# A four-layer graph network on one core: fewer barriers between the first two convolutions, and a rearranged final stage

## What is computed

```python
h = sage_mean(x, src, dst, W_self1, W_neigh1, b1, n)   # x @ W_self + mean of neighbours @ W_neigh + b
h = relu(h)
h = sage_mean(h, src, dst, W_self2, W_neigh2, b2, n)   # the second convolution
...
# last layer, agg being the sum of the neighbours' rows
h = (1.0 + gin_eps[0]) * x + agg
h = h @ W.T + b
mean = jnp.mean(h, axis=0)
var = jnp.mean(jnp.square(h - mean), axis=0)
h = gamma * (h - mean) * jax.lax.rsqrt(var + BN_EPS) + beta
h = jax.nn.relu(h) + x
out = layernorm(x + h)                                  # so twice x is added to the relu
```

## Time and profile before

| what | us |
|---|---|
| median of three runs | 1755.76 |
| their range | 1755.16 to 1755.86 |
| the profiled execution | 1752.44 |
| its span, first to last instruction | 1750.3 |
| PE busy | 1468.5 |
| DVE, ACT, POOL busy | 760.0, 668.9, 784.7 |

### The profile page before, as it was taken

How to read it: one execution, slowest core, us unless ns; L and a number is a source line. 1 busy time by engine, 2 the same in 40 slices (tenths; PEclk the granted TensorE clock), 3 DMA queues, 4 the chain that set the end, 5 groups by cost and what they waited for, 6 DMA issues and landing times.

```text
span 1750.3 us, 31633 instructions
## 1 busy us (share of the span) xinstructions
PE 1468.5 (84%) x9759; PEld 1049.2 (60%) x9872; DVE 760.0 (43%) x2792; ACT 668.9 (38%) x1236; POOL 784.7 (45%) x819
## 2 busy tenths in 40 slices
PE   1789999969986877888888888889888988957996
PEld 1346666644545766676666666667666766634554
DVE  6997888622333322233334334323433343235445
ACT  3765555520002433344335334434433453321111
POOL 4300000000003777777777777777777777710000
PEclk9999999989997999989999999999999999969998
DMA  2000000001005333333333333333333333300001
GB/s 78 1 0 1 2 1 1 2 25 38 0 0 158 98 82 82 82 86 83 82 80 87 83 82 80 88 79 85 84 82 82 83 86 82 74 11 1 1 1 38
DMA packets 158697, 95.81 MB, mean 55 GB/s; under 512 B 120584, under 2 KB 143879, under 8 KB 158607
## 3 DMA queue, kind: packets, MB, share of 16 engines
q0 software_dynamic: 25088, 51.43, 11.4%
q1 hardware_dynamic: 133519, 43.21, 10.0%
HBM read 87.24 MB, written 7.32 MB: 54 GB/s over the span
## 4 chain that ended last, share of the span: by engine, by line
PE 31%; DMA 11%; POOL 9%; issue 8%; DVE 5%; ACT 2%; DVEq 2%; SPq 1%; POOLq 0%; ACTq 0%
DMA arena<-x_w1a,idx 9%; POOL arena L751 9%; PE ps L1077 6%; PE ps L1217 6%; PE ps L1086 5%; PE ps L1070 4%; PE ps L1058 3%; PE ps L1066 3%; PE ps L1127 1%; PE ps L1201 1%; DVE arena L1986 1%; DVEq L328 1%; DMA arena<-in_edge_attr 1%; DVE idx L1955 1%; ACT arena L1490 1%
## 5 line engine op out<-in xcount | busy, mean ns | idle before, releaser
L751 POOL DMA_INDIRECT arena<-x_w1a,idx x784 | 742.3, 947 | 692.2 <-issue 651.9
L1480 ACT ACTIVATE arena<-ps 88x512 f32<-88x512 f32 x196 | 116.3, 594 | 478.9 <-PE ps L1058 473.4
L1086 PEld LDWEIGHTS ps<-arena 128*128 128x128 f32 x1568 | 208.4, 195 | 111.5 <-issue 74.0
L1066 PE MATMUL ps<-ident_f,arena 128*128 128x128 f32 x784 | 132.6, 294 | 110.4 <-DMA arena<-x_w1a,idx 109.7
L1986 DVE TENSOR_TENSOR arena<-ps,bias_b 128x512 f32<-128x512 f32 x196 | 135.6, 692 | 204.6 <-PE ps L1077 204.6
L1981 DVE TENSOR_TENSOR arena<-win_i,late 128x96 f32<-128x96 f32 x196 | 51.4, 262 | 391.5 <-PE ps L1086 380.7
L1077 PE MATMUL ps<-w_c,arena 128*128 128x128 f32 x1568 | 221.3, 287 | 0.0
L1319 ACT ACTIVATE adj<-ps 128x300 f32 x392 | 172.5, 450 | 125.2 <-PE ps L815 118.1
L1070 PE MATMUL ps<-arena 88*128 88x512 f32 x392 | 208.3, 613 | 3.7 <-ACT arena L1480 3.7
L1077 PEld LDWEIGHTS ps<-w_c,arena 128*128 128x128 f32 x1568 | 204.4, 203 | 0.2
L1086 PE MATMUL ps<-arena 128*128 128x24 f32 x1568 | 197.0, 264 | 5.3 <-ACT arena L1490 2.9
(11 more groups left out here) (187 smaller groups left out, 1447.0 us busy)
## 6 DMA issues: line engine op xcount, KB each, us to landing
arena<-in_edge_attr SPq DMA_DIRECT2D x196, 128.0 KB, 2.5
arena<-x_w1a,idx POOLq DMA_INDIRECT x784
arena<-x_w1b SPq DMA_DIRECT2D x196, 12.0 KB
x_spill<-arena SPq DMA_DIRECT2D x1, 1600.0 KB, 7.2
x_w1a<-arena SPq DMA_DIRECT2D x6, 256.0 KB, 2.3
x_w1b<-arena SPq DMA_DIRECT2D x6, 256.0 KB, 2.6
arena<-x_spill SPq DMA_DIRECT2D x6, 256.0 KB, 2.8
out_x<-arena SPq DMA_DIRECT2D x3, 512.0 KB
```

Source lines behind the costliest of these rows:

```text
L751: pool.indirect_dma_start(out=z_e[v][:, j * D:(j + 1) * D], out_offset=None, in_=xa_d[:, :], in_offset=bass.IndirectOffsetOnAxis(ap=idx[:, ...
L1066: pe.matmul(z_t[:, j * P:(j + 1) * P], z_e[v][:, j * P:(j + 1) * P], ident_f[:, :], is_transpose=True, start=(j == 0), stop=False)
L1086: last = pe.matmul(ps[:, WIN_BANK[v % 2], 0:WIN], msg[:, j * P:(j + 1) * P], oh_e[v][:, j, :], start=(j == 0), stop=(j == J - 1))
```

## The change

At the seam: barriers 2 and 3 move into the If body. In the Else body the steps run on semaphores alone: PE's sums of chunk 6 and the two linear steps come behind the branch, the split of `xn` is written out chunk by chunk on ACT (`h_hi`, `h_mid`) and DVE (`h_less_hi`, `h_low`) with buffers of its own (`res_1`), with the relus and combines of chunks 5 and 6 between them. The flag's transpose goes to bank 0 after the first 24 terms of chunk 5's sums, the square root of the degrees comes earlier on ACT, `late` is reloaded when the adjacency is written, the second weights and bias are loaded when PE and DVE no longer need the first ones, and the loop of conv 2 has its first pair written out.

At the end: batch-norm rows go to `z_t` (the memory of `acc`), so that `xn` stays; barrier 8 is gone. Each chunk has a PSUM bank of its own, and PE adds twice the fp32 rows with one matmul a chunk (`twice_x`) as soon as that bank is read. Relu goes by chunks, statistics by chunks, and of a pair's two chunks DVE normalizes the first and ACT the second.

```diff
-            for n in range(1, 3):
-                phase_end(sp, n)
+            phase_end(sp, 1)
+            sp.wait_ge(adj_written, counted(ROUNDS))
...
+            with sp.Else():
+                sp.wait_ge(c1_lin, NC)
+                second_weights()
+                sp.wait_ge(c1_done, NC)
+                second_bias()
+                sp.wait_ge(res_ready, 2 * NC)
+                sp.sem_inc(phase_ends, 2)
             load_nodes(xn, t["x"], loads[3])
             phase_end(sp, 4)
...
-            phase_end(sp, 8)
-
             for g, (k0, nt) in enumerate(PAIR):
-                sp.wait_ge(out_ready, g + 1)
+                sp.wait_ge(out_ready, min(2 * g + 2, NC))
...
-            c1_sum(EARLY, ALL_TERMS)
+            c1_sum(EARLY, ALL_TERMS[:24])
             pe.wait_ge(off_ready, 1)
-            pe.transpose(ps[0:1, 3, 0:P], off[:, 0:1], ident_f[:, :]).then_inc(off_t, 1)
+            pe.transpose(ps[0:1, 0, 0:P], off[:, 0:1], ident_f[:, :]).then_inc(off_t, 1)
+            c1_sum(EARLY, ALL_TERMS[24:])
             for c in (EARLY, EARLY + 1):
                 for j in range(CHUNKS[c][1]):
                     c1_own(c, j)
-            c1_sum(EARLY + 1, ALL_TERMS)
-            c1_linear(EARLY)
-            c1_linear(EARLY + 1)
-            phase_end(pe, 2)
...
             def sage(call, c, nt):
                 n0 = call * NC
+                pe.wait_ge(loads[4], 48 * (call + 1))
...
+                c1_sum(EARLY + 1, ALL_TERMS)
+                c1_linear(EARLY)
+                c1_linear(EARLY + 1)
+                layer(1, sage, aggregate, peeled=1)
+                pe.sem_inc(phase_ends, 2)
             phase_end(pe, 4)
...
-            phase_end(pe, 8)
-
             pe.wait_ge(twice_ready, 1)
-            for g, (k0, nt) in enumerate(PAIR):
-                pe.wait_ge(bn_relu, g + 1)
-                if g >= 2:
-                    pe.wait_ge(out_ready, g - 1)
+
+            def twice_x(c):
+                k0, nt = CHUNKS[c]
+                pe.wait_ge(gin_out, c + 1)
+                pe.matmul(ps[:, c, 0:nt * D], twice_i, xn[:, k0:k0 + nt, :].rearrange("p k d -> p (k d)"),
+                          start=True, stop=False)
+
+            def add_bn(c):
+                k0, nt = CHUNKS[c]
+                pe.wait_ge(bn_relu, c + 1)
                 for j in range(nt):
-                    k = k0 + j
-                    o = ps[:, 2 * (g % 2) + j // CH, (j % CH) * D:(j % CH + 1) * D]
-                    for q in range(3):
-                        pe.matmul(o, ident_h[:, :], parts[q][:, k, :], start=(q == 0), stop=False)
-                    last = pe.matmul(o, agg_all[:, k * P:(k + 1) * P], ident_f[:, :], start=False, stop=True)
+                    last = pe.matmul(ps[:, c, j * D:(j + 1) * D], z_t[:, (k0 + j) * P:(k0 + j + 1) * P], ident_f[:, :],
+                                     start=False, stop=(j == nt - 1))
                 last.then_inc(fin_ready, 1)
+
+            for c in range(4):
+                twice_x(c)
+            for c in range(NC):
+                add_bn(c)
+                if c + 4 < NC:
+                    twice_x(c + 4)
...
+            act.wait_ge(deg_ready, 1)
+            act.activation(std_deg[:, :], dinv[:, :], ACT.Sqrt).then_inc(deg_ready, 1)
             c1_copy(EARLY, 1)
             c1_copy(EARLY, 0)
             c1_copy(EARLY + 1, 0)
-            c1_copy(EARLY + 1, 1)
-            act.wait_ge(deg_ready, 1)
-            act.activation(std_deg[:, :], dinv[:, :], ACT.Sqrt).then_inc(deg_ready, 1)
-            c1_relu(EARLY)
-            c1_relu(EARLY + 1)
-            phase_end(act, 2)
...
+            def h_hi(c):
+                k0, nt = CHUNKS[c]
+                act.wait_ge(c1_relued, c + 1)
+                act.activation(parts[0][:, k0:k0 + nt, :], xn[:, k0:k0 + nt, :], ACT.Copy).then_inc(hi_ready, 1)
+
+            def h_mid(c):
+                k0, nt = CHUNKS[c]
+                act.wait_ge(res_ready, NC + c + 1)
+                act.activation(parts[1][:, k0:k0 + nt, :], res_1[c % 2][:, 0:nt, :], ACT.Copy).then_inc(mid_ready, 1)
...
+            with act.Else():
+                act.sem_inc(self_out, NC)
+                c1_copy(EARLY + 1, 1)
+                act.wait_ge(c1_own_ready, NC)
+                h_hi(0)
+                h_hi(1)
+                h_mid(0)
+                h_mid(1)
+                for c in range(2, EARLY):
+                    h_hi(c)
+                for c in range(EARLY, NC):
+                    c1_relu(c)
+                for c in range(2, EARLY):
+                    h_mid(c)
+                for c in range(EARLY, NC):
+                    h_hi(c)
+                    h_mid(c)
+                act.sem_inc(phase_ends, 2)
...
-            phase_end(act, 8)
-
-            for k0, nt in PAIR:
-                act.activation(agg_all[:, k0 * P:(k0 + nt) * P], agg_all[:, k0 * P:(k0 + nt) * P], ACT.Relu,
+            act.wait_ge(cols_ready, 2)
+            for k0, nt in CHUNKS:
+                act.activation(z_t[:, k0 * P:(k0 + nt) * P], z_t[:, k0 * P:(k0 + nt) * P], ACT.Relu,
                                bias=cols[:, 6:7], scale=cols[:, 5:6]).then_inc(bn_relu, 1)
-            for k0, nt in PAIR:
+            for g, (k0, nt) in enumerate(PAIR):
                 root(nt)
+                if nt == 2 * CH:
+                    act.wait_ge(fin_norm, g + 1)
+                    for j in range(CH, nt):
+                        last = act.activation(xn[:, k0 + j, :], ps[:, 2 * g + 1, (j - CH) * D:(j - CH + 1) * D], ACT.Identity,
+                                              scale=rstd[:, j:j + 1], bias=nbias[:, j:j + 1])
+                    last.then_inc(out_ready, 1)
...
+                h_less_hi(0)
+                h_less_hi(1)
+                h_low(0)
+                h_low(1)
+                c1_combine(EARLY)
+                c1_combine(EARLY + 1)
+                for c in range(2, NC, 2):
+                    some = range(c, min(c + 2, NC))
+                    for n in some:
+                        h_less_hi(n)
+                    for n in some:
+                        h_low(n)
...
+                dve.tensor_scalar(twice_i, ident_f[:, :], 2.0, None, ALU.mult).then_inc(twice_ready, 1)
...
-            phase_end(dve, 8)
-
-            dve.tensor_scalar(ident_h[:, :], ident_h[:, :], 2.0, None, ALU.mult).then_inc(twice_ready, 1)
+            dve.tensor_tensor(cols[:, 6:7], cols[:, 2:3], rstd[:, 1:2], ALU.subtract).then_inc(cols_ready, 1)
+
+            def rows_of(c, nt):
+                return ps[:, c, 0:nt * D].rearrange("p (j d) -> p j d", d=D)
+
             for g, (k0, nt) in enumerate(PAIR):
-                dve.wait_ge(fin_ready, g + 1)
-                b = 2 * (g % 2)
-                layernorm(ps[:, b:b + 2, :].rearrange("p a (j d) -> p (a j) d", d=D), xn[:, k0:k0 + nt, :], nt, done=out_ready)
+                halves = [(2 * g, CH), (2 * g + 1, CH)] if nt == 2 * CH else [(2 * g, nt)]
+                for c, n in halves:
+                    dve.wait_ge(fin_ready, c + 1)
+                    for j in range(n):
+                        own.add(dve.bn_stats(stats[:, CH * (c - 2 * g) + j, :], rows_of(c, n)[:, j, :]))
+                own.wait()
+                if g:
+                    dve.wait_ge(out_ready, 2 * g)
+                for j in range(nt):
+                    last = dve.bn_aggr(mv[:, j, :], stats[:, j, :])
+                last.then_inc(var_ready, 1)
+                roots[0] += 1
+                dve.wait_ge(std_ready, roots[0])
+                own.add(dve.reciprocal(rstd[:, 0:nt], std[:, 0:nt]))
+                own.wait()
+                if nt == 2 * CH:
+                    dve.scalar_tensor_tensor(out=nbias[:, 0:nt], in0=mv[:, 0:nt, 0], scalar=-1.0, in1=rstd[:, 0:nt],
+                                             op0=ALU.mult, op1=ALU.mult).then_inc(fin_norm, 1)
+                c, n = halves[0]
+                for j in range(n):
+                    last = dve.tensor_scalar(xn[:, k0 + j, :], rows_of(c, n)[:, j, :], mv[:, j, 0:1], rstd[:, j:j + 1],
+                                             ALU.subtract, ALU.mult)
+                    if j < n - 1:
+                        own.add(last)
+                last.then_inc(out_ready, 1)
```

More of the change, by code:

```diff
@@ L731, in _ @@
             with pool.If_ne(flag, 0):
+                phase_end(pool, 2)
                 for n in (1, 2):
@@ L736, in _ @@
                 scan(pool, X, scan_tile)
-            phase_end(pool, 3)
-            with pool.If_ne(flag, 0):
+                phase_end(pool, 3)
                 scan(pool, H, scan_tile)
+            with pool.Else():
+                pool.sem_inc(phase_ends, 2)
             phase_end(pool, 4)
@@ L1438, in relu_pair @@
                     p0, pt = PAIR[g]
[L1439 to L1451 removed]
+                    act.activation(xn[:, p0:p0 + pt, :], node[:, 0:pt, :], ACT.Relu).then_inc(c1_relued, 1)
             def root_pair(times):
@@ L1458, in root_pair @@
                 return roots_of
-            split(1)
```

(38 more changed lines are left out.)

81 lines of the change are left out of this document (42 added, 39 removed).

## The result

| | before | after |
|---|---|---|
| median, us (four runs of each, side by side) | 1755.46 | 1733.12 |
| their range | 1752.97 to 1755.86 | 1732.42 to 1739.08 |
| the profiled execution | 1752.44 | 1732.96 |
| its span | 1750.3 | 1730.8 |

The forecast had 1736.7 (1730 to 1742.5).

What follows compares the result with a forecast made beforehand. Most of the span is the untouched edge loop, so time before and after it counts one for one. Savings of 11.8 + 7.3 = 19.1 us from the profiled 1752.44 give 1733.3; plus 3.3 for the median, 1736.7 (range 1730 to 1742.5).

Steps and rivals of the forecast that it cites:

- The seam: Between convolutions 1 and 2: 11.8 us saved, conv 2 starting at 384.85 at full clock against 396.66.
- Run-ahead: PE's sequencer runs 17 matmuls ahead at the seam, reaching the flag load at 370.05, 1.2 us ahead.
- Rival A: At the seam PE's jump is hidden by a longer queue, with no idle or half clock: 1731.1, chance 0.17.
- Price of the jump: PE's branch between the rows and chunk 6's sums costs 3.97 us, the late transfer being out of its way.
- Half clock: PE's restart behind the jump loses 2.0 us in the sums of chunk 6, with ends 0 and 4.35.
- The chain to conv 2: After chunk 6's sums: ACT's copy and high part, DVE's residuals, the low part, with gaps 3.2 us.
- The stall for low part 2: Early in conv 2, low part 2 comes some 0.4 us after PE wants it; 0.4 added.
- The end: Final stage behind batch norm's last factor: early doublings, chunk-wise steps and ACT's share save 7.3 us.
- Rival C: PE runs the end at half clock, chunk 1 at 1730.7 rather than 1724.95: 5.8 lost, 1742.5, chance 0.06.
- B: Slow seam restart: jump 5.74, chunk 6's sums and conv 2's first 16 matmuls at half clock; 1743.6, chance 0.17.
- D: Conv 2 stays at half clock, 0.22 us more per 512-column matmul; 1769.7 at a third of them; chance 0.02.
- E: At the seam SP's queue (weights, bias, x) holds conv 2 back; only 7.3 is left, 1748.5, chance 0.03.

Runs made afterwards that it cites:

- e0: The changed kernel run again with no edit, beside before on one chip: 1734.08 us, ratio 0.9891.
- e1: Only the hunks between the convolutions, against the kernel before, with the final stage as before: 1740.72 us, ratio 0.9938.
- e6: The changed kernel, but the doubling of each chunk waits for ACT's relu of that chunk: 1736.54 us, ratio 0.9902 to before.
- e7: The changed kernel, but DVE normalizes both chunks of a pair and ACT has no share: 1738.44 us, ratio 0.9908 to before.
- e4: The kernel before with one edit: SP starts the late reload when the adjacency is written, ahead of barrier 2: 1751.32 us, ratio 0.999.
- e3_jump_early: The changed kernel with PE's flag load and jump moved ahead of 25 of chunk 5's last 50 sums: 1726.70 us, ratio 0.9857 to before.
- e5: The changed kernel with the late reload started so that it runs during PE's jump: 1734.01 us, ratio 0.9895 to before.
- e2_end: Only the hunks of the final stage, against the kernel before, with barriers 2 and 3 kept: 1743.16 us, ratio 0.9954.

## Why the prediction was right, point by point

**The seam** was forecast at 11.8 us. In the first profile it is 23.54 - 11.19 = 12.35 of the distance and 18.84 - 16.37 = 2.47 in conv 2's first matmuls, 14.8. Over the five profiles in which the seam is as the change has it (after, e0, e1, e6, e7) the distance is 12.33 on the mean, so the gain 13.7. Of it the reload's way out of the jump accounts for 1.85 (e4); the rest came with the barriers and the new order of the steps, which no run took apart. The steps:
- *Run-ahead.* Load at 370.05 expected, 369.84 seen; the 17 matmuls hold, and e3_jump_early shows the queue a second time. Rival A falls by this. TensorE: Matmul & The Clock Gate in the Trainium skill gives the queue 64 entries; here the sequencer stood 18 matmuls ahead, 36 instructions with their weight loads, which is less, and no run shows what set this number.
- *Price of the jump.* Taken as 3.97; it was 3.32 to 3.86 in these five. The step of choosing between the rows by the reload was right (e4, e5); the term was 0.1 to 0.65 too high. Advanced Engine Details and Errata, section Control Flow Timing, in the Trainium skill has 108 ns for a compare-and-branch; none of the twelve jumps of the table comes near.
- *Half clock.* Taken as 2.0, with 0 and 4.35 as ends. It was 0 in two of the five and 1.62 in three. This is the mis-sized term for the first profile; for the kernel it was a fair value, only not a constant.
- *The chain to conv 2.* 3.2 us expected from the end of the sums to conv 2, 3.1 to 3.3 seen in the five (378.36 to 381.66 in after). The stall for low part 2: 0.4 expected, 0.22 seen (e0_again, where the trace has all 75 matmuls of that sum: the 25th starts 0.44 us behind the 24th, the others 0.22 apart).

**The end** was forecast at 7.3 us, and is 8.0 (25.75 to 17.79). The pair was 4.5 on paper and 4.31 on the chip, twice in a row; ACT's 1.5 was 1.51. E6 and e7 show two parts: without the early doublings 2.4 us are lost, without ACT 3.5. The 2.1 left, with barrier 8 gone, fewer matmuls in each add, and relu and statistics by chunks, no run took apart. Rival C did not come: PE ran at granted clock 1.00 through the adds (1709 to 1717). Its price of 5.8 was too high, since in e6 the half clock lasted 3.4 us, not all the way.

**What the sum did not have.** By these sizes 13.7 + 8.0 = 21.7 us should have gone, and 19.1 to 20.7 did. The forecast let time before the edge loop count one for one, and about 1.3 us of the difference lies just there: the projection took 26.6 to 27.0 us in all six profiles with the jump between the rows and the sums, 25.2 to 26.2 in the three with barriers. In after POOL's branch ahead of the first gather is at 533.24, 3.26 us after the last store of x W1a was issued; in before it was 1.73. In the DMA records of the six a 16 KB instruction fetch runs 20.7 to 23.4 us behind conv 2's last matmul, beside these stores, where the other six profiles have one at about 12. That the fetch is the cause is argued, not shown: no run moved it alone. The rest is scatter of the edge loop, 979.0 to 982.5 us from the first gather to the last in the twelve, and of the tail. In ten of the twelve the tail goes with its stretches at half clock: 192.1 to 192.5 us at 34.1, 194.2 to 194.6 at 37.5, 194.9 at 41.0; before (193.5 at 34.6) and e2_end (193.1 at 30.7) lie outside of that row. The first two profiles side by side: the seam and conv 2 give 14.5 and the end 8.0, the projection takes back 1.4, the edge loop and the tail 0.7 each, other stretches 0.2, and 19.5 are left of the span. The gain of e3_jump_early over the changed kernel can be split the same way: against the mean of the five its seam is 12.33 - 8.41 = 3.9 us shorter (2.9 against after alone, 4.7 to 5.0 against those with the half clock), its projection 1.9; that is 5.8 of the 6.0, less the short breaks in chunk 5's sums. That they agree so closely is luck, given the 4 us on either side.

**The base.** I added 3.3 us since the median of before stood that far above its profiled run. With more runs before came to 1752.0 to 1753.1, where the profile was. That step was wrong, and it is why the forecast lay above the result: 1752.44 less 19.1 is 1733.3. That this is so near the measured 1733.12 is in part luck: the seam gave about 1.9 more than its sum and the end 0.7, and the stretches behind the seam took about as much back.

The rivals: A and B ask for a break of none and for sums wholly at half clock; neither showed. Conv 2 ran at granted clock 1.00 from 378 to 505, so D falls; its start moved by 12, so E falls.

## What to carry to other kernels

An engine's jump over unused code is paid in the open, here with 2.5 to 3.1 us, if little work is queued behind which to hide it: put it ahead of long instructions, count how many the sequencer runs ahead, and keep large transfers away from it. Work that doesn't depend on the last result (here the doublings) can be worth more ahead of a wait than its own length, since it also held the clock here (2.4 us in e6, for a doubling of 0.86). Price a restart at half clock as a range with both ends, and take the base of a forecast from many runs.

## What the runs showed of the hardware that I had not expected

- The same stretch of code, with a break of 2.5 to 3.1 us on PE, kept granted clock 1.00 in two profiles and fell to 0.50 in three, 0.9 to 1.3 us after PE had begun to work again. Breaks of 2.53 and 2.54 kept the clock, 2.67, 3.05 and 3.13 (and 3.79 in e5) lost it for 3.4 us, 1.62 us of time each.
- A jump of one engine costs more while another queue's transfer runs: 5.54 and 5.74 us with the reload just issued, 3.74 with only that taken away, 4.59 with it put back in another place. In all twelve profiles the jump ended 1.34 to 1.42 us after its 16 KB instruction fetch had landed, and the reload moved the start of that fetch from 1.0 to as much as 3.3 us into the jump.
